# Score and exponent products in 64-row halves, on two rings of three PSUM banks

## What is computed

```python
xn = layernorm(x)
Q, K, V = xn @ W_q + b_q, xn @ W_k + b_k, xn @ W_v + b_v          # 16 heads of 8 features
scores = (Q_h K_h^T + relative term of |k - q| clipped at 2) / sqrt(8), causal mask
attn = softmax(scores);  out = attn @ V_h + relative value term
x = x + layernorm(out @ W_o + b_o)
f = layernorm(x)
shared = silu(f @ sw1) * (f @ sw3) @ sw2
routed = sum over the best 2 of 8 experts of gate_e * gelu(f @ ew1[e]) @ ew2[e]
x = x + layernorm(shared + routed)
```

## Time and profile before

| | |
|---|---|
| median of 3 runs | 1222.0 us (1219.4 to 1222.1) |
| the profiled execution | 1219.6 us, span 1217.9 us |
| TensorE, VectorE busy | 1045.1 us (86%), 913.1 us (75%) |
| ScalarE, GpSimd busy | 720.2 us (59%), 719.8 us (59%) |
| mean granted TensorE clock | 0.96 |

### The profile page before, as it was taken

The page is one execution under the profiler, slowest core; times in us unless marked ns, Lnnn a source line. Parts: engine busy times, 40 slices in busy tenths (PEclk is TensorE's granted clock), DMA queues, the critical chain, the costliest instruction groups (busy, mean ns, idle before and its releaser), DMA issues. The chain is left out here.

```text
span 1217.9 us, 27718 instructions
## 1 busy us (share of the span) xinstructions
PE 1045.1 (86%) x7527; PEld 609.6 (50%) x7527; DVE 913.1 (75%) x1998; ACT 720.2 (59%) x1625; POOL 719.8 (59%) x1063
## 2 busy tenths in 40 slices
PE   1369999899989989998998999999865899999996
PEld 0134445354444535444453454544323777777774
DVE  3686887768868777886877778787736888888884
ACT  2316666566656656665665666666733567766674
POOL 2104555546556455654645566464554688898887
PEclk9779999999999999999999999999986899999999
DMA  5100101101010010101001010010131354444541
GB/s 150 35 21 17 36 14 34 37 10 43 8 40 17 29 41 6 45 13 34 29 17 45 4 43 24 22 43 3 58 101 46 122 166 154 158 150 149 168 153 42
DMA packets 61439, 70.80 MB, mean 58 GB/s; under 512 B 9505, under 2 KB 39073, under 8 KB 61345
## 3 DMA queue, kind: packets, MB, share of 16 engines
q1 hardware_dynamic: 61344, 69.47, 18.0%
HBM read 43.75 MB, written 8.65 MB: 43 GB/s over the span
## 5 line engine op out<-in xcount | busy, mean ns | idle before, releaser
L705 ACT ACTIVATE prob<-ps_exp 128x512 f32<-128x512 f32 (+3 forms) x1024 | 411.3, 435 | 258.2 <-PE ps_exp L1366 255.5
L1014 DVE TENSOR_REDUCE mx<-ps_wide 128x2 f32<-128x256 f32 (+3 forms) x512 | 409.5, 819 | 150.0 <-PE ps_wide L1386 147.8
L585 POOL TENSOR_SCALAR_AFFINE_SELECT prob<-prob 128x258 f32<-128x258 f32 (+1 forms) x512 | 220.2, 455 | 135.2 <-ACT prob L705 132.8
L1366 PE MATMUL ps_exp<-qs,ks 128*128 128x512 f16 (+3 forms) x1024 | 268.5, 306 | 31.1 <-issue 16.5
L1383 PE MATMUL ps_wide<-ks,qs 126*128 126x128 f16 (+3 forms) x1024 | 231.3, 308 | 53.4 <-DVE mx L1014 32.2
L666 POOL TENSOR_TENSOR hidden_low<-hidden,hidden_high 128x512 fp32r<-128x512 f32 x144 | 190.5, 1345 | 26.8 <-ACT hidden_high L873 25.6
L1403 PE MATMUL ps_av<-prob,vp 128*32 128x512 f32 (+3 forms) x2048 | 195.9, 455 | 4.0 <-POOL prob L585 3.0
L1383 PEld LDWEIGHTS ps_wide<-ks,qs 126*128 126x128 f16 x1024 | 71.3, 100 | 202.9 <-issue 111.9
L1386 PE MATMUL ps_wide<-maskb,identb 128*128 128x129 bf16 (+1 forms) x1024 | 145.2, 223 | 0.0
L1366 PEld LDWEIGHTS ps_exp<-qs,ks 128*128 128x128 f16 x1024 | 91.1, 97 | 99.3 <-ACT prob L705 61.1
L602 POOL TENSOR_TENSOR v_near<-v_near,p 128x256 f32<-128x256 f32 x64 | 41.4, 667 | 150.9 <-ACT p L782 150.9
(11 more groups left out here) (168 smaller groups left out, 1704.4 us busy)
## 6 DMA issues: line engine op xcount, KB each, us to landing
gate_rows<-gates_dram SPq DMA_DIRECT2D x128, 256.0 KB, 3.3
qs<-qh SPq DMA_DIRECT2D x128, 32.0 KB
qs<-ql SPq DMA_DIRECT2D x128, 32.0 KB
ks<-kh SPq DMA_DIRECT2D x128, 32.0 KB
ks<-kl SPq DMA_DIRECT2D x128, 32.0 KB
xnT_dram<-oT SPq DMA_DIRECT2D x16, 256.0 KB, 2.0
xeT<-xnT_dram SPq DMA_DIRECT2D x16, 256.0 KB, 2.7
out<-result SPq DMA_DIRECT2D x16, 256.0 KB, 2.3
```

The costliest lines, as they stand in the source:

```text
L585: pool.affine_select(out=v, in_=v, compare_op=ALU.is_ge, fill=0.0, base=-2, pattern=[[0, 2], [1, w]], channel_multiplier=-1).then_inc(S["p ...
L705: act.activation(prob[pr % PBUF][:, b, START[kt]:START[kt] + w], ps_exp[b][:, 0:w], ACT.Exp, scale=SCALE).then_inc(S["exp_done"], 1)
L1014: dve.tensor_reduce(mx[:, qt, 2 * pr:2 * pr + 2], ps_wide[unit][:, :, 0:P * (qt + 1)], AX.X, ALU.max).then_inc(wide_free[unit], 1)
L1366: pe.matmul(ps_exp[b][:, 0:w], ks[par][b][:, pr, P * kt:P * kt + P], qs[par][:, pr, P * kt:SEQ], start=True, stop=True).then_inc(S["exp_fu ...
```

## The change

- **Rows.** `ks` is one tensor for both heads. A score or exponent product contracts 63 or 64 rows, rows 0 to 63 for b = 0 and 64 to 127 for b = 1, both with 128 columns of the array. The maximum's row is 63 or 127. The mask product is cut in halves of 64 rows too: `identb`/`maskb` and their copies with the halves swapped, `identr`/`maskr`, are both added for each head, four matmuls where two stood.
- **Banks.** `ps_exp` (2 banks) and `ps_wide` (2 x 2) become two rings of three single banks: `ps_s` for scores, `v0`, `v1`, `q`, `k`, `oproj`; `ps_e` for exponents, `xT`, `oT`.
- **Units.** A unit is one head and one full bank of 512 columns: `E_UNITS` and `S_UNITS` pack the tiles of two pairs into five units per head. A step has 20 rounds (5 in each of 4 groups) with two exponent and two score units each: 40 evictions by ScalarE for 64, 40 maxima for 32. Units of tiles with several widths give more than one partial maximum, and `max_half` has one more small reduction.
- **Masks of the exponents**: 5 affine selects of 516 or 256 columns per group for 8 of 256 or 258.
- **TensorE's other work**: `v` and `qk` are cut in two, 12 visits of `av_part` for 16, new places in all lists.

```diff
-SLOTS = NPAIR * NT * 2
-AT = {"av2": 3, "e_sums": 6, "m1": 8, "s_tok": 13, "av3": 19, "v": 20, "xT": 24, "oT": 28,
-      "oproj": 32, "qk": 36, "av0": 38, "m0": 42, "av1": 54, "xn2": 57, "logits": 59}
...
+E_UNITS = [[(0, 0, 0)], [(0, 1, 0), (0, 3, 384)], [(0, 2, 0), (1, 2, 256)], [(1, 0, 0)], [(1, 1, 0), (1, 3, 384)]]
+S_UNITS = [[(0, 3, 0)], [(0, 0, 0), (0, 2, 128)], [(0, 1, 0), (1, 1, 256)], [(1, 3, 0)], [(1, 0, 0), (1, 2, 128)]]
+NU = len(E_UNITS)
+ROUNDS = NU * NGRP
...
+AT = {"e_sums": 0, "av2": 1, "m1": 2, "s_tok": 3, "v0": 5, "v1": 6, "av3": 6, "xT": 7, "oT": 9, "q": 10,
+      "av0": 11, "oproj": 11, "k": 12, "m0": 13, "av1": 16, "xn2": 18, "logits": 19}
...
-            ks0 = [sb_attention(f"ks0{b}", [P, NPAIR, SEQ], F16) for b in range(2)]
-            prob = [sb_attention(f"prob{i}", [P, 2, PCOLS]) for i in range(PBUF)]
+            ks0 = sb_attention("ks0", [P, NPAIR, SEQ], F16)
+            sb_attention("apart", [P, NPAIR, SEQ], F16)
+            prob = [sb_attention(f"prob{i}", [P, NU, 2, SEQ]) for i in range(2)]
...
-        ps_exp = [ctx.enter_context(nc.psum_tensor(f"ps_exp{i}", [P, SEQ], F32)) for i in range(2)]
-        ps_wide = [ctx.enter_context(nc.psum_tensor(f"ps_wide{i}", [P, 2, SEQ], F32)) for i in range(2)]
+        ps_e = [ctx.enter_context(nc.psum_tensor(f"ps_e{i}", [P, SEQ], F32)) for i in range(RING)]
+        ps_s = [ctx.enter_context(nc.psum_tensor(f"ps_s{i}", [P, SEQ], F32)) for i in range(RING)]
...
-                masks(8, 16)
+                masks(3, 10)
...
-                masks(16, 25)
+                masks(10, 13)
+                if st.A:
+                    near_half(st, st.a, 0)
+                masks(13, 15)
                 if st.C:
                     normalise(st, st.c, xn2[:, :, :], tiles(xr[:, st.seq(st.c), :]), mv3, var3, rs3,
                               "stats3").then_inc(S["xn2_ready"], 1)
-                if st.A:
-                    near_half(st, st.a, 0)
-                masks(25, 32)
+                masks(15, 20)
...
+                own.mark(dve.tensor_reduce(mx[:, 2, hs], mx[:, 4:13:4, hs].rearrange("p r h -> p h r"), AX.X, ALU.max))
...
-                maxima(19, 21)
+                maxima(24, 27)
                 if st.F:
                     split(st)
-                maxima(21, 22)
-                if st.C:
-                    x1_bn(st)
-                maxima(22, 24)
-                if st.C:
-                    aggregate(st3, mv3, "stats3")
-                maxima(24, 25)
+                maxima(27, 29)
                 if st.F:
                     near_products(st)
                 if st.t0 == 0:
                     buffers(1)
-                maxima(25, 27)
+                maxima(29, 31)
+                if st.C:
+                    x1_bn(st)
+                maxima(31, 33)
+                if st.C:
+                    aggregate(st3, mv3, "stats3")
                 if st.B:
                     av_tok_out(st, st.b, 1)
-                maxima(27, 32)
+                maxima(33, 40)
...
+            def exp_unit(st, i):
+                g, u, b = i // (2 * NU), i % (2 * NU) // 2, i % 2
+                par, rows = st.b % 2, slice(HALF * b, HALF * b + HALF)
+                scores = e_bank(st, f"e{i}")
+                if i % HALF_UNITS == 0:
+                    pe.wait_ge(mrow[i // HALF_UNITS], st.at(32 * (st.b + 1), 32))
+                for off, kt, at in E_UNITS[u]:
+                    pr = 2 * g + off
+                    last = pe.matmul(scores[:, at:at + WIDTH[kt]], ks[par][rows, pr, P * kt:P * kt + P],
+                                     qs[par][rows, pr, P * kt:SEQ], start=True, stop=True)
+                last.then_inc(S["e_full"], 1)
...
+            def s_masks(u, both, n):
+                _, qt, at = S_UNITS[u][n]
+                lo, hi = at + max(P * (qt + 1) - DIAG, 0), at + P * (qt + 1)
+                last = [None, None]
+                for eye, far in ((identb, maskb), (identr, maskr)):
+                    for b in (1, 0):
+                        rows = slice(HALF * b, HALF * b + HALF)
+                        last[b] = pe.matmul(both[b][:, lo:hi], eye[rows, :], far[rows, DIAG - (hi - lo):DIAG],
+                                            start=False, stop=eye is identr)
...
+                for r in range(ROUNDS):
+                    g, u = r // NU, r % NU
+                    for what, use in uses.items():
+                        if AT[what] == r and here[STAGE[what]]:
+                            use()
+                    both = [None, None]
                     if st.B:
-                        exp_unit(st, pr, n)
-                    for what, use in uses.items():
-                        if AT[what] == slot and here[STAGE[what]]:
-                            use()
-                    if n % 4 == 1:
-                        kt = pr % 2 * 2 + n // 4
-                        if pr >= 2 and st.B:
-                            av_part(st, st.b, pr // 2 - 1, kt)
-                        if pr < 2 and st.C:
+                        exp_unit(st, 2 * r)
+                    if st.A:
+                        both[1] = s_unit(st, 2 * r)
+                    if st.B:
+                        exp_unit(st, 2 * r + 1)
+                    if st.A:
+                        both[0] = s_unit(st, 2 * r + 1)
+                        s_masks(u, both, 0)
+                        for n in range(1, len(S_UNITS[u])):
+                            for i in range(2):
+                                s_part(st, 2 * r + i, both[1 - i], n)
+                            s_masks(u, both, n)
+                    for kt in {2: (0,), 3: (1,), 4: (2, 3)}.get(u, ()):
```

More of the change, by code:

```diff
@@ L32, with ring_order @@
 WIDTH = [SEQ - P * kt for kt in range(NT)]
-START = [sum(WIDTH[:kt]) for kt in range(NT)]
-PCOLS = sum(WIDTH)
-SLOTS = NPAIR * NT * 2
-AT = {"av2": 3, "e_sums": 6, "m1": 8, "s_tok": 13, "av3": 19, "v": 20, "xT": 24, "oT": 28,
-      "oproj": 32, "qk": 36, "av0": 38, "m0": 42, "av1": 54, "xn2": 57, "logits": 59}
[L41 to L47, removed]
+E_UNITS = [[(0, 0, 0)], [(0, 1, 0), (0, 3, 384)], [(0, 2, 0), (1, 2, 256)], [(1, 0, 0)], [(1, 1, 0), (1, 3, 384)]]
+S_UNITS = [[(0, 3, 0)], [(0, 0, 0), (0, 2, 128)], [(0, 1, 0), (1, 1, 256)], [(1, 3, 0)], [(1, 0, 0), (1, 2, 128)]]
+NU = len(E_UNITS)
+ROUNDS = NU * NGRP
+NUNIT = 2 * ROUNDS
+HALF_UNITS = NUNIT // 2
+PROB_AT = {(pr, kt): (u, at) for u, parts in enumerate(E_UNITS) for pr, kt, at in parts}
+AT = {"e_sums": 0, "av2": 1, "m1": 2, "s_tok": 3, "v0": 5, "v1": 6, "av3": 6, "xT": 7, "oT": 9, "q": 10,
+      "av0": 11, "oproj": 11, "k": 12, "m0": 13, "av1": 16, "xn2": 18, "logits": 19}
+STAGE = {"av2": "C", "e_sums": "A", "m1": "B", "s_tok": "A", "av3": "C", "v0": "A", "v1": "A", "oT": "C", "xT": "F",
+         "oproj": "C", "q": "F", "k": "F", "av0": "B", "m0": "A", "av1": "B", "xn2": "C", "logits": "C"}
+STAGE.update({f"s{i}": "A" for i in range(NUNIT)})
+STAGE.update({f"e{i}": "B" for i in range(NUNIT)})
+def ring_order(uses, units):
+    return [what for _, what in sorted([(2 * AT[w] - 0.5, w) for w in uses] + [(i, f"{units}{i}") for i in range(NUNIT)])]
+S_RING = ring_order(("v0", "v1", "q", "oproj", "k"), "s")
+E_RING = ring_order(("xT", "oT"), "e")
+RING = 3
+MISC_ORDER = sorted((w for w in AT if w not in S_RING + E_RING), key=AT.get)
 LOOP0, LOOP_STEPS = 3, NSEQ - 4 - (NSEQ - 4) % 2
-CHAIN_DVE, CHAIN_POOL = 39, 14
+CHAIN_DVE, CHAIN_POOL = 40, 14
 class Step:
@@ L78, in misc, with s_use, s_turn, e_use @@
         return self.at(self._uses(MISC_ORDER, what), len(MISC_ORDER))
[L80 to L88, removed]
+    def s_use(self, what):
+        n = self._uses(S_RING, what)
+        return self.at(n, len(S_RING)), n % RING
+    def s_turn(self, what):
+        return self.at(self._uses(S_RING, what) // RING, len(S_RING) // RING)
+    def e_use(self, what):
+        n = self._uses(E_RING, what)
+        return self.at(n, len(E_RING)), n % RING
+    def e_turn(self, what):
+        return self.at(self._uses(E_RING, what) + 1 - RING, len(E_RING))
+    def e_past(self):
+        return self.at(sum(self._on(t)[STAGE[w]] for t in range(self.t0) for w in E_RING), len(E_RING))
 def steps(eng, body):
@@ L907, in buffers @@
             def buffers(i):
[L909 to L910 removed]
+                dve.memset(ks[i][:, :, :].bitcast(F32), 0.0).then_inc(S["k_zeros"], 1)
                 dve.memset(qs[i][:, :, :].bitcast(F32), 0.0).then_inc(S["q_rows"], 1)
@@ L1201, in step @@
                     gates_second(0, EARLY)
-                maxima(12, 16)
+                maxima(13, 22)
                 if st.C:
                     y_out(st)
-                maxima(16, 17)
+                if st.A:
+                    max_half(st, st.a, 0)
+                maxima(22, 23)
                 if st.C:
                     y_bn(st)
-                maxima(17, 18)
+                if st.B:
+                    av_tok_out(st, st.b, 0)
+                maxima(23, 24)
                 if st.C:
```

(9 more changed lines are left out.)

382 lines of the change are left out of this document (191 added, 191 removed).

## The result

The changed kernel takes **1294.79 us** in the median of 4 runs (1292.7 to 1299.14), against 1221.71 us for the kernel before on the same chip: ratio **1.060**, 95% interval 1.058 to 1.063. It is 73 us slower; the forecast was 1169 us, with a range whose upper end was to take in the clock case of 1233 us, and it is missed by 126 us. The profiled execution has a span of 1293.8 us.

A forecast was written before the change was run, and what follows sets the result against it. Neither engine was full before, with 5.4 us of hand-over; afterwards VectorE binds: 44.3 plus 3.8 waits makes 48.1 a step. 15 x (51.3 - 48.1) = 48, and 5: 1222 - 53 = 1169 us; range from 1117, a little widened, to include 1233.

The forecast's parts named there:

- the clock case: Rival, chance 0.07: TensorE idles more, a fifth of each full step runs at 1.2 GHz; 1233 us.
- What it still waits for: VectorE's remaining waits in a full step: 2.8 us at the xn2 transposes, 1.0 for rounds with value visits.
- residual of 3.8 us: Total VectorE waiting left in a full step, added to its 44.3 us to give 48.1.
- 5.4 us of hand-over: Part of a full step before the change, from in-order queues with only two units of scores between TensorE and VectorE.
- three banks hold one maximum more: Score banks between TensorE and VectorE; used in setting value-visit waits at 1.0 us a step.
- the forecast's 3.2 us a step: Gain of each full step, from 51.3 us to 48.1 us, over 15 steps.
- the rival that they don't (0.15): Rival, chance 0.15: products in different row halves don't overlap on TensorE, so the kernel is slower, 1262 to 1319 us.
- 7.2 us a step: TensorE time saved on score and exponent products by running row halves side by side, 17.8 us down to 10.6.
- 1.8 for masks: TensorE time added by 128 half-height mask products for 64 full ones, range 0 to +3.7 us a step.
- 1.9 for height: TensorE time added by full-height work between 64-row products in 15 of 20 rounds, range 0 to +3.75 us.
- the 3.75 of the upper bound: Highest TensorE cost a step for changes of height, due in full if changing tile size drains the array.
- Step 17: The step with exponents and no scores, 41 us before; forecast to fall by 5 us (0 to -8).

The follow-up runs named there:

- e3: The changed kernel with ScalarE's small evictions (av_s, s_rows, qf, v_out) moved ahead by one or two exponents each, nothing added or left out; 1273.28 us.
- e4: The changed kernel with small producers moved ahead in both ScalarE's and VectorE's lists, second statistics by four maxima; 1242.1 us.
- e6: e4 with four score banks and two exponent banks, one half of v moved to the misc bank, the other a round later; 1203.74 us.
- e12: The changed kernel plus one batch of four unused products a round in rounds 12 to 16, nothing else; 1336.29 us.
- e9: e6 plus one batch of four unused TensorE products a round in rounds 12 to 16; 1189.45 us.
- e1: The changed kernel with score and exponent products over all rows again and masks as 128-row products, so other output; 1347.44 us.

## Why the prediction was wrong

**The step that failed** is "What it still waits for", with its residual of 3.8 us: 2.8 at the xn2 transposes and 1.0 for value visits, which replaced the 5.4 us of hand-over found before. Measured are 13.1 us of waits at the maxima and 1.2 at the o product. The forecast took the new lists as being smooth except at one place. It had read off how many slots lie between a producer and its consumer for xn2 alone; five others (av_s, s_rows, num, qf, v_near) came out at a round or less, each a standstill of 0.5 to 1.5 us with all scores and exponents behind it. Over the 15 full steps TensorE waits 73.4 us, 4.9 a step, at these five, and at xn2 only 1.3 a step (19.5 us) where 2.8 was forecast. e3 and e4 show what it costs: re-ordering, with no work taken away, gives back 53 us. e4 moves the second statistics too, so its 31 us hold some of the xn2 wait.

**The second miss is the same step's ring.** I held that "three banks hold one maximum more" and would hide most. During the split VectorE frees no bank for 4 us, and TensorE runs dry. e6 gives the ring a fourth bank, moves half of v out of it and gains 38 us.

**The third is the clock**, which I had as a rival of chance 0.07 and 1233 us. It fell as that rival said, to 0.88 in full steps from 0.99. Since the clock has two levels, 0.88 in the mean is 24% of the time at 1.2 GHz (0.12 / 0.5), near the "fifth" of the rival; but I had added it to 5.4 us of hand-over, while it comes with the larger waits: in e4 it fell right behind one. In e6 filling them up gave 14 us. What it costs in the change as it stands was not isolated: e12 raised it by 0.02 alone and cost 41 us.

1294.8 less 53 (lists), 38 (ring) and 14 (filled waits) is 1189, e9's time; since each kernel builds on the last, this is no test of the parts. 20 us still lie between this and 1169, and the waits that are left hold them. Maxima and q evictions in e9:

```profile
L1065 DVE TENSOR_REDUCE mx<-ps_s 128x4 f32<-128x512 f32 (+2 forms) x396 | 255.3, 682 | 77.4 <-PE ps_s L1456 76.3
```
```profile
L766 ACT ACTIVATE qf<-ps_s,bq x16: 687/687/688, 29.8 to 758.1; 128x512 f32<-128x512 f32 x16
```

The q evictions are 728.3 / 15 = 48.6 us apart; the forecast's 3.2 us a step off the 50.6 of before makes 47.4, and 1.2 us in 15 steps is 17 us. The maxima still wait 7.7 us a step (76.3 in 9.9 steps) where 3.8 was forecast; which of these waits could go was not tried.

**What was right.** The halves run side by side, and the rival that they don't (0.15) is out: the kernel landed within that rival's 1262 to 1319 us for another reason. Their gain was forecast as 7.2 us a step, less 1.8 for masks and 1.9 for height and so 3.5 net, and e1 measures 53 / 15 = 3.5; e1 has a higher clock (0.93 to 0.88) and the masks of one height, so this agreement is partly luck. The change of height at 1.9 was sized well: transposes between 64-row products start 0.15 us behind the last mask, where the next mask would start after 0.06, and take 0.59 for 0.44 (677.82, 677.97 and 678.56 us), 0.24 in all. That is as much as a value visit already paid, and 7 of the 15 rounds with such work don't follow a visit: an estimate of 1.7 us a step, not the 3.75 of the upper bound. VectorE: 0.684 us a maximum, 40 a step, 40.6 us busy for 41.8. Masks: pairs of half masks start at the same hundredth and four take two slots of 0.06 us, so the lower bound of +0 is nearer than the 1.8 I took. Step 17: -5 us, as forecast. The feed-forward stage at nothing: right.

**The signs that I had named.** Starts within 0.02 us: yes. Maxima at 0.68: yes. VectorE above 85% busy in full steps: no, 70% (351.0 of 500). The four mask products 0.03 apart in the mean: yes. TensorE's longest waits at xn2: no, at score banks (39.5 us) and spread over six small consumers. Clock under 0.95: yes, which I had given as a sign of being wrong. A step above 50 us: yes (56.6), but with VectorE waiting for score banks to be filled and hardly for the stacks' DMAs; TensorE's waits for them come to 2.8 us in all full steps.

## What to carry to other kernels

When work on an in-order queue is made shorter, list every consumer at which that queue can stop and count, in each producer's own list, how far ahead it stands; one such wait estimated and five forgotten cost as much here as the halves gained, some 50 us. Choose the depth of a ring by the longest piece of its consumer that frees no bank, not by the mean. And when TensorE gets idler, look at its granted clock: a part of what is saved can go again in stretches at half speed, and idle time that can't be removed may be worth filling, though here it paid only after the hand-overs were mended (e9 against e12).

## What the runs showed of the hardware

- TensorE's granted clock dropped to 0.50 for 10.3 us after a stretch in which it was busy for 7.2 of 11.7 us, with a standstill of 2.81 us behind VectorE's split at its end (e4). Unused products in the rounds with such waits raised the mean in 500 us from 0.88 to 0.98, with a kernel 14 us faster (e6, e9).
- Two 64-row products in different row halves and different banks start at the same hundredth of a microsecond; four of 512 columns take 0.45 us, where two over all rows took 0.44.
- A change between 64-row and 128-row products costs some 0.1 us each way (0.22 for a mask pair in place of 0.12, 0.27 for 384 columns in place of 0.16).
